# Delta-rule recurrence: the first leaf computed from the contact banks in four pieces, the last decayed W written in place, and P of the even leaves scaled on GpSimd with its products ahead of Q's

## The chip, the cores and the metric

The kernel runs on one core of a Trainium2 chip. The metric is device time in microseconds (us) of one execution, the median of several runs. Engines are named as in the profile: PE is TensorE's matmul, PEld its weight load, DVE is VectorE, ACT is ScalarE, POOL is GpSimd, SPq is the DMA queue of SyncE.

## The reference, cut to what matters

A transformer block on one sequence of 2048 tokens of width 256: layer norm, attention, a residual sum, layer norm, a mixture of experts, a residual sum. The change lies in the attention's recurrence alone (the change also touches how the first stage counts its weight buffers). There are 16 heads; each keeps a 128 by 128 state S that is decayed, corrected and read once a token:

```python
q = silu(dwconv_causal(x @ Wq, ...)); k = ...; v = ...      # (T, 16, 128) each
a = sigmoid(x @ Wa + ba)                                     # (T, 16, 128)
beta = sigmoid(x @ Wb + bb)                                  # (T, 16)
def step(S, t):
    y = einsum('bhvk,bhk->bhv', S, k_t * SCALE)
    err = y - v_t
    S = a_t[..., None] * S - (b_t[..., None] * err)[..., None] * k_t[:, :, None, :]
    o = einsum('bhvk,bhk->bhv', S, q_t)
    return (S, o)
```

## The kernel before, in words

Three stages follow one another. Stage A projects the tokens and convolves them (to about 636 us of the trace), stage B is the recurrence (`recurrence`, 636 to 2758 us), stage C is the feed-forward part. Everything is float32.

**Chunks and leaves.** Stage B walks through 32 chunks (`g`) of 64 tokens for all 16 heads at once, each chunk in 16 leaves (`j`) of 4 tokens. Each engine has its own program, in a fixed order written out by hand; the engines meet through counting semaphores (`wait(engine, count, chunk, k)`), and an engine that waits holds back all that stands behind it in its program. [...]

**Start of a chunk.** PE multiplies the state by the keys and queries of the whole chunk ("contact", 32 matmul records into four PSUM banks, four heads each). `contact_copy` on ACT copies each bank to SBUF, to `P` (the part that belongs to the keys) and `Qs[g % 2]` (the part of the queries). When all four copies are done (`cont`), DVE starts the first leaf.

**A leaf on DVE** (`chunk` in the vector block, L1137 to L1147). A product in place in the leaf's coefficients `NC` (L1137: `left` is the first leaf's P or, from the second leaf on, the sums in the PSUM tile `psM`), a reduction into the solved rows `W` (L1140), and a product with the decays of the leaf (L1147) into `WR` (even leaves), `WT` (odd leaves) or `WC`, which shares its memory with `WE` (the larger merges).

**Behind it.** PE transposes the decayed rows into `psT` (L1723), ACT copies them to `WL`, and PE forms in `psM` what the next tokens need: `WL` times masked products of the keys (`OWN` for an even leaf, `BD` for an odd one, which merges 2, 4 or 8 leaves) plus P and Q of the next tokens, brought in by a product with the identity (L1735, L1739). For an even leaf P and Q are handled together: `pair(g)` is a view of both, DVE scales both by the leaf's decay in one instruction (`scale_leaf`, L1100, 128x128), and two matmuls of 128 columns (two records each, since they are float32) fill `psM` (L1733 and L1735; for the first leaf L1739 and L1741). The next leaf's L1137 waits for both. ACT then copies the rest of P (`rest_copy`, count `prc`) or the leaf's Q (`leaf_q_copy`) out of `psM`.

**DVE's other work in a leaf**, in the order of its program: `add_merged` (L1114), `scale_leaf` (L1100), `scale_leaf_w` (L1105), and then masks, row products and `leaf_solution` of the half chunk to come (L1023), spread over the leaves by hand.

**POOL's program** (`chunk` order in the gpsimd block): `scale_right` (L879 for P and Q of a merge of two leaves, L887 for the larger ones, one instruction for P and one for Q), `scale_left` (L899), `decayed_q` (L850), `gate` (L860), `row_decays` (L830), `block_decays` (L816) and `decayed_w` (L838 to L843). `past(g, j)` is a wait: for an even leaf until DVE has done `scale_leaf_w` (L1105), for an odd one until L1147. In leaf 6 the program reads: `decayed_q`, `gate`, `scale_right(g, 7, (0,))`, `scale_left(g, 5)`, `scale_left(g, 7)`.

**End of a chunk.** After the last leaf ACT copies the last four decayed leaves into `WE`, PE transposes `WE` (L1767), ACT copies that to `WTOK`, PE forms the update of the state (L1665), DVE adds it (L1087), and the next contact begins (L1558). Odd chunks also carry the output projection `wo` of two chunks on PE (L1628, L1688), partly ahead of the merge products of leaf 14.

Every engine's copies on ACT share the line L1244. The kernel text:

Of the kernel before, what the change touches and what calls it, by code (L numbers as in the profile page):

```python
# [10 lines left out]
H, D = 16, 128  # L11
# [57 lines left out]
def project_inputs(nc, ident, x_d, wb_d, bb_d, wpack_d, scr, nbeta_d):  # L69
# [3 lines left out]
    with ctx:  # L73
# [48 lines left out]
        def _(sp):  # L122
# [18 lines left out]
            def heads(t, last):  # L141
                for s in range(2):
# [58 lines left out]
        def _(dve):  # L201
# [45 lines left out]
            c_used[0].start(dve)  # L247
            c_used[1].start(dve)
            with dve.Fori(0, TURNS) as t:
                for s in range(2):  # L250
# [18 lines left out]
                    dve.sem_inc(c_used[s].sem, 1)  # L269

        @block.scalar
        def _(act):
# [43 lines left out]
            for c in (*ag_free, *ca_used):  # L316
                c.start(act)

            with act.Fori(0, TURNS) as t:
                for s in range(2):  # L320
# [35 lines left out]
                    act.sem_inc(ca_used[s].sem, 1)  # L356

        @block.tensor
        def _(pe):
# [31 lines left out]
            w_used[0].start(pe)  # L391
            w_used[1].start(pe)
# [112 lines left out]
def recurrence(nc, ident, scr, nbeta_d, wo_d, lng_d, lnb_d, att_d):  # L505
# [9 lines left out]
    with ctx:  # L515
# [85 lines left out]
        ap = Count(sem("leaf_terms"), J)  # L601
        ws = Count(sem("w_solved"), J, 1, 1)
        wt = Count(sem("w_decayed"), J)
        psc, psc0 = Count(sem("pq_scaled"), JM - 1), Count(sem("leaf_pq_scaled"), JM // 2 + 1)
# [29 lines left out]
        def taken(g, kind, *rest):  # L634
# [13 lines left out]
            return {"contact": (cont, g, n + 1), "ktok": (ktok, g, n + 1), "decay": (stg, g, n + 1),  # L648
# [113 lines left out]
        def _(pool):  # L762
# [125 lines left out]

            def scale_left(g, j):
# [80 lines left out]
        def _(dve):  # L970
# [144 lines left out]

            def chunk(g):
                here, nxt = 2 * g + 1, 2 * g + 2
                more = g + 1 < NCH
                for j in range(J):
# [6 lines left out]
                    if j == 0:  # L1126
                        wait(dve, cont, g, 4)

                        wait(dve, awm, g - 1, 3)
                        wait(dve, wxc, g - 1, 1)  # L1130
                        left = P[:, :, 0:R]
                    else:
                        wait(dve, mps, g, 2 * j - 1)
                        n = merge_of(j - 1)[1]
                        at = H * R * at_p(g) if j % 2 else 0
                        left = psM[:, at:at + H * n].rearrange("p (h t) -> p h t", h=H)[:, :, 0:R]
                    tt(eq[:, :, :, 1:5], eq[:, :, :, 1:5], left.unsqueeze(2).to_broadcast([128, H, R, R]), ALU.mult)\  # L1137
                        .then_inc(ap.sem, 1)
                    wait(dve, ap, g, j + 1)
                    nc.vector.tensor_reduce(W[:, :, lf], eq, AXIS.X, ALU.add).then_inc(ws.sem, 1)  # L1140
                    wait(dve, ws, g, j + 1)
# [1051 lines left out]
```

## Time and profile before

| | |
|---|---|
| median of three runs | 3103.65 us (3093.4 to 3106.2) |
| the profiled execution, span from first to last instruction | 3102.6 us |
| its own time beside the span | the times given are 3106.2, 3103.65 and 3093.4 us; the span lies among them, 1.05 us under the median |
| busy in that span | PE 88%, PEld 60%, DVE 72%, ACT 52%, POOL 44% |
| stage B | 2122 us of the span |

Busy shares are those of the whole span; an engine counts as busy while an instruction of it runs, waiting for an operand port included. A row of the timeline has the start in us, the time it takes in us, the engine, the line of the kernel and the instruction, merged with its like (xN); in brackets is the idle time of the engine before it and who ended it.

### The profile page before, as it was taken

Reading aid. Unit: us, or ns where it says so; the run is one execution under the profiler, and the core shown is the slowest. Engines: PE = TensorE matmul, PEld = TensorE weight load, DVE = VectorE, ACT = ScalarE, POOL = GpSimd, SP = SyncE. Lnnn points to the kernel's source line nnn. Section 1 sums busy time; section 2 is a strip of 40 time slices with the busy share of each in tenths; the row PEclk is TensorE's granted clock in tenths of the full one; section 3 lists DMA queues with packets and bytes.
Section 4 is the critical chain, followed back from the end, with each engine's and each line's share of the span. In section 5 each row is a group of like instructions: output and inputs, shape, how many; then the busy total and the mean of one; then the engine's idle time right before and its main releaser. Section 6 shows DMA issues by size and latency. Waiting matters only on the chain. (4 is left out here: it accounts for less than half of the span.)

```text
span 3102.6 us, 48417 instructions
## 1 busy us (share of the span) xinstructions
PE 2732.2 (88%) x14144; PEld 1863.5 (60%) x14144; DVE 2239.8 (72%) x4680; ACT 1610.3 (52%) x3516; POOL 1377.8 (44%) x1760
## 2 busy tenths in 40 slices
PE   7999999768898888988889888898888888859999
PEld 3555555446666666666666666666666666635555
DVE  6777777677888878888788887888887888623332
ACT  6666666545555555555555555555555555412111
POOL 3666676734544445444454444544445444310000
PEclk9999999989999999999999999999999999979999
DMA  3655556533232232322323223232223222034120
GB/s 124 241 225 206 233 230 239 196 82 67 43 57 42 44 65 47 57 42 43 64 49 57 42 44 59 53 57 42 44 51 61 46 53 43 9 107 109 45 38 14
DMA packets 449883, 261.22 MB, mean 84 GB/s; under 512 B 402672, under 2 KB 414672, under 8 KB 447472
## 3 DMA queue, kind: packets, MB, share of 16 engines
q1 hardware_dynamic: 449664, 258.51, 31.5%
q8 instruction: 112, 1.84, 0.3%
q14 instruction: 107, 0.88, 0.1%
HBM read 153.42 MB, written 105.05 MB: 83 GB/s over the span
## 5 line engine op out<-in xcount | busy, mean ns | idle before, releaser
L265 DVE SCALAR_TENSOR_TENSOR A_acc<-A_psY,A_w,A_acc 128x410 f32<-128x410 f32 (+1 forms) x720 | 419.2, 637 | 151.6 <-ACT A_acc L334 151.6
L405 PE MATMUL A_psY<-A_xT,A_w 128*128 128x413 f32 (+1 forms) x960 | 347.2, 510 | 9.1 <-PE A_psAG L411 7.7
L1244 ACT ACTIVATE B_PQ<-B_psM 128x64 f32<-128x64 f32 (+2 forms) x480 | 125.2, 261 | 441.2 <-DVE B_NC L1137 440.9
L1137 DVE TENSOR_TENSOR B_NC<-B_NC,B_psM 128x256 f32<-128x256 f32 x480 | 200.8, 418 | 182.5 <-PE B_psM L1756 92.8
L192 POOL TENSOR_TENSOR A_outs<-A_outs,A_acc 128x410 f32<-128x410 f32 (+1 forms) x240 | 229.7, 987 | 216.1 <-ACT A_outs L342 216.1
L899 POOL TENSOR_TENSOR B_WT<-B_WT,B_G 128x128 f32<-128x128 f32 (+2 forms) x224 | 143.4, 640 | 371.2 <-ACT B_WT L1244 184.3
L1244 ACT ACTIVATE B_WL<-B_psT 64x128 f32<-64x128 f32 (+3 forms) x480 | 148.5, 309 | 265.6 <-PE B_psT L1723 265.4
L405 PEld LDWEIGHTS A_psY<-A_xT,A_w 128*128 128x128 f32 x960 | 180.2, 189 | 165.5 <-issue 164.2
L1140 DVE TENSOR_REDUCE B_W<-B_NC 128x64 f32<-128x320 f32 x512 | 248.7, 486 | 17.6
L334 ACT ACTIVATE A_acc<-A_psY,A_w 128x410 f32<-128x410 f32 (+1 forms) x240 | 166.1, 692 | 162.9 <-PE A_psY L405 161.2
L879 POOL TENSOR_TENSOR B_PQ<-B_PQ,B_G 128x256 f32<-128x256 f32 x128 | 89.4, 699 | 345.5 <-DVE B_WT L1105 345.5
L1756 PE MATMUL B_psM<-B_BD,B_WL 128*128 128x128 f32 x1536 | 228.2, 288 | 12.4 <-ACT B_WL L1244 4.6
L1756 PEld LDWEIGHTS B_psM<-B_BD,B_WL 128*128 128x128 f32 x1536 | 192.5, 192 | 71.9 <-ACT B_WL L1244 69.5
L411 PE MATMUL A_psAG<-A_xT,A_w 128*128 128x410 f32 (+1 forms) x640 | 233.1, 506 | 0.0
L887 POOL TENSOR_TENSOR B_PQ<-B_PQ,B_G 128x256 f32<-128x256 f32 (+1 forms) x192 | 159.6, 845 | 128.3 <-DVE B_WE L1147 127.6
L1023 DVE TENSOR_TENSOR B_NC<-B_NC,B_TMP 128x384 f32<-128x384 f32 (+1 forms) x192 | 184.7, 962 | 3.3
L411 PEld LDWEIGHTS A_psAG<-A_xT,A_w 128*128 128x128 f32 x640 | 120.9, 189 | 99.6 <-issue 99.6
L1568 PE MATMUL B_ring<-B_KQ,B_KL 128*128 128x256 f32 x512 | 139.5, 396 | 25.4 <-DMA B_KQ<-scr 25.3
L1733 PE MATMUL B_psM<-B_OWN,B_WL 64*128 64x128 f32 x448 | 106.7, 319 | 51.7 <-ACT B_WL L1244 51.7
L2048 ACT ACTIVATE C_act_g<-C_psG 128x512 f32<-128x512 f32 (+1 forms) x56 | 33.4, 597 | 228.3 <-PE C_psU L2103 228.3
L1723 PE MATMUL B_psT<-ident,B_WR 128*64 128x128 f32 x256 | 75.7, 296 | 86.3 <-DVE B_WR L1147 85.1
L850 POOL TENSOR_TENSOR B_SQ<-B_PQ,B_E 128x256 f32<-128x256 f32 x128 | 129.4, 1012 | 47.0 <-DVE B_WT L1147 45.6
(207 smaller groups left out, 6588.4 us busy)
## 6 DMA issues: line engine op xcount, KB each, us to landing
B_KQ<-scr SPq DMA_DIRECT2D x96, 512.0 KB, 6.6
scr<-A_outs SPq DMA_DIRECT2D x48, 615.0 KB, 3.5
scr<-A_outag SPq DMA_DIRECT2D x32, 615.0 KB, 5.2
scr<-A_outs SPq DMA_DIRECT2D x48, 409.0 KB, 2.5
A_xc<-nbeta SPq DMA_DIRECT2D x16, 1024.0 KB, 5.9
B_A<-scr SPq DMA_DIRECT2D x32, 512.0 KB, 4.6
B_C<-scr SPq DMA_DIRECT2D x32, 512.0 KB, 6.3
B_G<-scr SPq DMA_DIRECT2D x32, 512.0 KB, 4.6
```

The lines of the kernel that those rows point to most:

```text
L192: nc.gpsimd.tensor_tensor(o, o, acc[:, p, n % 2, 0:t1 - t0], ALU.mult).then_inc(silu[p].sem, 1)
L265: nc.vector.scalar_tensor_tensor(a, y, w[:, s, col:col + 1], a, ALU.mult, ALU.add)\
L334: nc.scalar.activation(acc[:, p, n % 2, 0:t1 - t0], psY[p][:, y0:y0 + t1 - t0], ACT.Identity, scale=w[:, s, col + HALO:col + HALO + 1], bi ...
L405: last = nc.tensor.matmul(psY[p][:, y0:y0 + HALO + t1 - t0], wp[:, p, kt, :], xT[:, kt, t0:t1 + HALO], start=kt == 0, stop=kt == KT - 1)
L411: last = nc.tensor.matmul(psAG[p][:, 0:t1 - t0], wp[:, A_ + p, kt, :], xT[:, kt, HALO + t0:HALO + t1], start=kt == 0, stop=kt == KT - 1)
L887: tt(x, x, gl.to_broadcast([128, H, n]), ALU.mult).then_inc(psc.sem, 1)
L899: tt(dst, dst, gr, ALU.mult).then_inc(wsc.sem, 1)
L1023: tt(out, in0, in1, op).then_inc(ncs.sem, 1)
L1137: tt(eq[:, :, :, 1:5], eq[:, :, :, 1:5], left.unsqueeze(2).to_broadcast([128, H, R, R]), ALU.mult)\
L1140: nc.vector.tensor_reduce(W[:, :, lf], eq, AXIS.X, ALU.add).then_inc(ws.sem, 1)
L1244: copy = lambda out, in_: nc.scalar.activation(out, in_, ACT.Copy)
L1756: last = mm(psM[:, 512 * q + rs * i:512 * q + rs * (i + 1)], WL[0:rs, 128 * i:128 * (i + 1)], BD[0:rs, bank, col + rs * part:col + rs * (p ...
```

## The change

In stage B:

- **First leaf in pieces.** `first_leaf` on DVE reads each contact bank straight from PSUM (four products of four heads) and reduces after the second and the fourth. ACT's copy of a bank now waits for DVE's product from that bank (`ap`), and a bank is free when both have read it.
- **Last decayed W in place.** L1147 of leaf 15 writes its place in `WE`; ACT's last copy takes three leaves instead of four and no longer waits for leaf 15; PE waits for L1147 instead.
- **Even leaves.** `scale_leaf` on DVE now scales Q alone (128x64). P is scaled on POOL by the new `scale_leaf_p`, placed at eight places of POOL's program (leaves 0, 2, ... 14); for j over 0 it waits for `rest_copy` of leaf j - 1. On PE two products of 128 columns become four of 64: identity times P and `WL` times `OWN` for P, then a semaphore that releases the next leaf, then the same for Q into the other PSUM bank.
- Counts of `ap` and `ws` shift by 3 and 1, with the waits on them.

In stage A the three semaphores on which the weight reload waits (`w_used`, `c_used`, `ca_used`) become one that counts to three.

The diff, cut to its core:

```diff
@@ stage A
-        w_used = [Count(sem(f"A_w_used{s}"), 1, 1, 1) for s in range(2)]
-        c_used = [Count(sem(f"A_c_used{s}"), 1, 1, 1) for s in range(2)]
-        ca_used = [Count(sem(f"A_ca_used{s}"), 1, 1, 1) for s in range(2)]
+        w_used = [Count(sem(f"A_w_used{s}"), 3) for s in range(2)]
...
@@ gpsimd
+            def scale_leaf_p(g, j):
+
+                wait(pool, dec, g, DEC)
+                wait(pool, prc, g, j // 2) if j else wait(pool, cont, g, 4)
+                x = P[:, :, R * (j + 1):R * (j + 2)]
+                tt(x, x, leaf_decay(g)[:, :, j:j + 1].to_broadcast([128, H, R]), ALU.mult).then_inc(psp.sem, 1)
...
                 more = g + 1 < NCH
+                scale_leaf_p(g, 0)
                 past(g, 0)
...
                     decayed_q(g - 1, 1)
+                scale_leaf_p(g, 2)
                 past(g, 2)
...
                     gate(g - 2, 2)
+                scale_leaf_p(g, 4)
                 past(g, 4)
...
                     gate(g - 2, 3)
+                scale_leaf_p(g, 6)
                 scale_right(g, 7, (0,))
                 scale_left(g, 5)
                 scale_left(g, 7)
...
                     row_decays(g + 1, 3)
+                scale_leaf_p(g, 8)
                 past(g, 8)
...
                     row_decays(g + 1, 5)
+                scale_leaf_p(g, 10)
                 past(g, 11)
                 scale_right(g, 11)
+                scale_leaf_p(g, 12)
                 past(g, 12)
                 scale_right(g, 13)
                 scale_left(g, 11)
+                scale_leaf_p(g, 14)
                 past(g, 14)
@@ vector
             def scale_leaf(g, j):
 
-                gl = leaf_decay(g)[:, :, j:j + 1].unsqueeze(1).to_broadcast([128, 2, H, R])
+                gl = leaf_decay(g)[:, :, j:j + 1].to_broadcast([128, H, R])
...
-                    wait(dve, prc, g, j // 2)
                     wait(dve, mq, g, j // 2)
-                x = pair(g)[:, :, :, r0:r0 + R]
+                x = Qs[g % 2][:, :, r0:r0 + R]
...
+            def first_leaf(g, eq):
+
+                for n in range(4):
+                    h = slice(4 * n, 4 * n + 4)
+                    left = take_bank(dve, g, "contact", n)[:].rearrange("p (h q t) -> p h q t", h=4, q=2)[:, :, at_p(g), 0:R]
+                    tt(eq[:, h, :, 1:5], eq[:, h, :, 1:5], left.unsqueeze(2).to_broadcast([128, 4, R, R]), ALU.mult)\
+                        .then_inc(ap.sem, 1)
+                    if n == 1:
+                        wait(dve, awm, g - 1, 3)
+                        wait(dve, wxc, g - 1, 1)
+                    if n % 2:
+                        half = slice(8 * (n // 2), 8 * (n // 2) + 8)
+                        wait(dve, ap, g, n + 1)
+                        nc.vector.tensor_reduce(W[:, half, 0:R], eq[:, half], AXIS.X, ALU.add).then_inc(ws.sem, 1)
...
-                    else:
-                        to = WT[:, j] if j % 2 else WR[:]
+                    elif j < JM:
+                        to = WT[:, j] if j % 2 else WR[:]
+                    else:
+                        wait(dve, tps, g, 12)
+                        to = WE[:, :, R * j:R * (j + 1)]
@@ scalar
                     ps = take_bank(act, g, "contact", i)
+                    wait(act, ap, g, i + 1)
...
-                wait(act, wt, g, J)
+                wait(act, wt, g, JM)
...
-                copy(w_end(12, J), w_leaves(12, J)).then_inc(wec.sem, 1)
+                copy(w_end(12, JM), w_leaves(12, JM)).then_inc(wec.sem, 1)
@@ tensor
                         if p == 0:
+                            wait(pe, psp, g, pair_number(j) + 1)
+                            mm(psM[:, 0:H * n], ident[:], P[:, :, r0:r0 + n], start=True, stop=False)
                             wait(pe, ow, g, 2 if j < 8 else 4)
-                            ...
+                            wait(pe, wl, g, j + 1)
+                            mm(psM[:, 0:H * n], WL[0:rs, 0:128], OWN[0:rs, j // 2, at_p(g), :, R:2 * R],
+                               start=False, stop=True).then_inc(mps.sem, 1)
+                            wait(pe, psc0, g, pair_number(j) + 1)
+                            mm(psM[:, 512:512 + H * n], ident[:], Qs[g % 2][:, :, r0:r0 + n], start=True, stop=False)
+                            mm(psM[:, 512:512 + H * n], WL[0:rs, 0:128], OWN[0:rs, j // 2, at_q(g), :, R:2 * R],
+                               start=False, stop=True).then_inc(mps.sem, 1)
...
                 wait(pe, wec, g, 2)
+                wait(pe, wt, g, J)
```

## Rows read from the trace of the kernel before

**Rows 1.** The page: the span and its instructions

```profile
span 3102.6 us, 48417 instructions
```

**Rows 2.** Stage B: length, busy PE, PEld, DVE, ACT, POOL, granted clock, DMA

```profile
636.00:2758.00 2122.00, 1842.62 (x11466) 1365.79 (x11464) 1671.93 (x3693) 1161.50 (x2724) 970.31 (x1311) 0.98 0.25 48
```

**Rows 3.** DVE's waits, 640 to 2700 us: total us, times, longest

```profile
DVE B_NC L1137 <- ACT B_PQ L1244: 60.8, 24, 2.9
DVE B_NC L1137 <- PE B_psM L1735: 40.3, 51, 1.2
DVE B_NC L1137 <- PE B_psM L1741: 33.0, 32, 3.2
```

**Rows 4.** Timeline: contact, leaf 0 and leaf 1 of a chunk

```profile
1613.62 0.60 ACT L1244 ACTIVATE B_PQ<-B_ring 128x512 f32<-128x512 f32 x1 [0.30 <-PE B_ring L1558]
...
1614.31 0.42 DVE L1137 TENSOR_TENSOR B_NC<-B_NC,B_PQ 128x256 f32<-128x256 f32 x1 [2.65 <-ACT B_PQ L1244]
1614.49 1.14 ACT L1355 ACTIVATE B_BD<-B_ring,B_E 128x128 f32<-128x128 f32 x4 [0.27 <-PE B_ring L1590]
...
1615.29 0.27 DVE L1147 TENSOR_TENSOR B_WR<-B_W,B_E 128x64 f32<-128x64 f32 x1
...
1615.94 0.27 ACT L1244 ACTIVATE B_WL<-B_psT 64x128 f32<-64x128 f32 x1 [0.31 <-PE B_psT L1723]
1616.02 0.67 POOL L879 TENSOR_TENSOR B_PQ<-B_PQ,B_G 128x256 f32<-128x256 f32 x1 [2.09 <-DVE B_WT L1105]
...
1616.36 0.34 PE L1741 MATMUL B_psM<-B_OWN,B_WL 64*128 64x128 f32 x1
...
1616.85 0.42 DVE L1137 TENSOR_TENSOR B_NC<-B_NC,B_psM 128x256 f32<-128x256 f32 x1 [0.96 <-PE B_psM L1741]
...
1617.83 0.27 DVE L1147 TENSOR_TENSOR B_WT<-B_W,B_E 128x64 f32<-128x64 f32 x1
1617.85 1.10 POOL L850 TENSOR_TENSOR B_SQ<-B_PQ,B_E 128x256 f32<-128x256 f32 x1
```

**Rows 5.** Timeline: leaf 6 of that chunk, to the start of leaf 7

```profile
1633.08 1.06 POOL L887 TENSOR_TENSOR B_PQ<-B_PQ,B_G 128x512 f32<-128x512 f32 x1
...
1633.25 0.40 DVE L1137 TENSOR_TENSOR B_NC<-B_NC,B_psM 128x256 f32<-128x256 f32 x1
...
1633.74 0.22 ACT L1244 ACTIVATE B_PQ<-B_psM 128x64 f32<-128x64 f32 x1 [1.49 <-DVE B_NC L1137]
...
1634.09 0.46 POOL L899 TENSOR_TENSOR B_WT<-B_WT,B_G 128x128 f32<-128x128 f32 x1
...
1634.20 0.47 DVE L1147 TENSOR_TENSOR B_WR<-B_W,B_E 128x64 f32<-128x64 f32 x1
...
1634.97 0.29 DVE L1100 TENSOR_TENSOR B_PQ<-B_PQ,B_E 128x128 f32<-128x128 f32 x1
...
1637.28 0.42 DVE L1137 TENSOR_TENSOR B_NC<-B_NC,B_psM 128x256 f32<-128x256 f32 x1
```

**Rows 6.** Timeline: L1147 of leaf 1 in another chunk, beside POOL

```profile
2138.01 1.10 DVE L1147 TENSOR_TENSOR B_WT<-B_W,B_E 128x64 f32<-128x64 f32 x1
2138.02 0.97 POOL L850 TENSOR_TENSOR B_SQ<-B_PQ,B_E 128x256 f32<-128x256 f32 x1
```

**Rows 7.** Groups by form, 640 to 2700 us: count, busy us, mean ns, idle

```profile
L1105 DVE TENSOR_TENSOR B_WT<-B_WR,B_E 128x64 f32<-128x64 f32 x254 | 55.3, 218 | 0.2
...
L816 POOL TENSOR_TENSOR B_G<-B_G 128x64 f32<-128x64 f32 x31 | 9.2, 298 | 2.4
```

**Rows 8.** Timeline: merge products of leaf 12 and start of leaf 13, odd chunk

```profile
1659.79 0.46 PE L1733 MATMUL B_psM<-B_OWN,B_WL 64*128 64x128 f32 x2 [0.45 <-ACT B_WL L1244]
...
1660.70 0.42 DVE L1137 TENSOR_TENSOR B_NC<-B_NC,B_psM 128x256 f32<-128x256 f32 x1 [0.99 <-PE B_psM L1735]
```

**Rows 9.** Timeline: ACT's last WE copy, even chunk; PE's transposes, odd chunk

```profile
1605.15 0.42 ACT L1244 ACTIVATE B_WE<-B_WT 128x256 f32<-128x256 f32 x1
...
1671.84 1.04 PE L1767 MATMUL B_psM<-ident,B_WE 128*128 128x128 f32 x8
```

More of the change, by code:

```diff
@@ L246, in _ @@
                 tap[p].start(dve)
-            c_used[0].start(dve)
-            c_used[1].start(dve)
             with dve.Fori(0, TURNS) as t:
@@ L268, in _ @@
                     dve.wait_ge(tap[2].sem, tap[2].at(t, 3 * (s + 1) * NTA))
[L269 removed]
+                    dve.sem_inc(w_used[s].sem, 1)
         @block.scalar
@@ L315, in _ @@
             nc.scalar.activation(nbeta[:], beta[:], ACT.Copy, scale=-SCALE * SCALE).then_inc(nbeta_sb, 1)
-            for c in (*ag_free, *ca_used):
+            for c in ag_free:
                 c.start(act)
@@ L390, in _ @@
             pe.wait_ge(beta_sb, T // 512)
-            w_used[0].start(pe)
-            w_used[1].start(pe)
             with pe.Fori(0, TURNS) as t:
@@ L600, in recurrence @@
         cont = Count(sem("contact_copied"), 4)
-        ap = Count(sem("leaf_terms"), J)
-        ws = Count(sem("w_solved"), J, 1, 1)
+        ap = Count(sem("leaf_terms"), J + 3)
+        ws = Count(sem("w_solved"), J + 1, 1, 1)
         wt = Count(sem("w_decayed"), J)
+        psp = Count(sem("leaf_p_scaled"), JM // 2 + 1)
         psc, psc0 = Count(sem("pq_scaled"), JM - 1), Count(sem("leaf_pq_scaled"), JM // 2 + 1)
@@ L647, in taken @@
                 return (am if n else atc, (g - 3) // 2, 1),
-            return {"contact": (cont, g, n + 1), "ktok": (ktok, g, n + 1), "decay": (stg, g, n + 1),
+            if kind == "contact":
+                return (cont, g, n + 1), (ap, g, n + 1)
+            return {"ktok": (ktok, g, n + 1), "decay": (stg, g, n + 1),
                     "update": (stu, g, n + 1), "oc": (oc, g - 1, n + 1),
@@ L1126, in chunk @@
                     if j == 0:
[L1127 to L1131, printed above, removed]
+                        first_leaf(g, eq)
                     else:
@@ L1134, in chunk @@
                         n = merge_of(j - 1)[1]
[L1135 to L1141, printed above, removed]
+                        left = psM[:, 0:H * n].rearrange("p (h t) -> p h t", h=H)[:, :, 0:R]
+                        tt(eq[:, :, :, 1:5], eq[:, :, :, 1:5], left.unsqueeze(2).to_broadcast([128, H, R, R]), ALU.mult)\
+                            .then_inc(ap.sem, 1)
+                        wait(dve, ap, g, j + 4)
+                        nc.vector.tensor_reduce(W[:, :, lf], eq, AXIS.X, ALU.add).then_inc(ws.sem, 1)
+                    wait(dve, ws, g, j + 2)
                     p, n, _ = merge_of(j)
@@ L1297, in leaf_diagonals @@
                         wait(act, zeros, 0, NZERO + 1)
-                    wait(act, ws, g - 1, 8 * h + 8)
+                    wait(act, ws, g - 1, 8 * h + 9)
                     copy(flat[:, :, 1], ones[:].to_broadcast([128, HJ2])).then_inc(nc0.sem, 1)
@@ L1363, in rest_copy @@
                 wait(act, mps, g, 2 * j + 1)
-                wait(act, ap, g, j + 2)
+                wait(act, ap, g, j + 5)
                 copy(P[:, :, r0 + R:r0 + n], m[:, :, R:n]).then_inc(prc.sem, 1)
             def leaf_q_copy(g, j):
-                m = psM[:, H * R * at_q(g):H * R * (at_q(g) + 1)].rearrange("p (h t) -> p h t", h=H)
+                m = psM[:, 512:512 + H * R].rearrange("p (h t) -> p h t", h=H)
                 wait(act, mps, g, 2 * j + 2)
-                wait(act, ap, g, j + 2)
+                wait(act, ap, g, j + 5)
                 copy(Qs[g % 2][:, :, R * (j + 1):R * (j + 2)], m).then_inc(mq0.sem, 1)
@@ L1716, in chunk @@
                         wait(pe, wl, g, j)
-                        wait(pe, ap, g, j + 1 if j else 0)
+                        wait(pe, ap, g, j + 4 if j else 0)
                         for i in range(tiles):
@@ L1761, in chunk @@
                         run_job(g, job)
-                wait(pe, ap, g, J)
+                wait(pe, ap, g, J + 3)
                 wait(pe, mq, g, JM // 2)
```

17 lines of the change are left out of this document (2 added, 15 removed).

## The prediction, made before the changed kernel ran

> **What bounds the kernel now.** I read the page first: the profiled execution spans 3102.6 us [rows 1], 1.05 us under the median of 3103.65 us, so I sum against 3102.6 and carry the sum to 3103.65 unchanged. The view by stretch puts 2122 us into stage B [rows 2]. The edit of stage A's semaphores leaves the same three conditions in front of the same load, so I cost it at 0, and all that follows is stage B: 32 chunks, 66.3 us each if the stretch is divided evenly. A gain of 1 us in a chunk is 32 us, 1%.
>
> Busy shares don't say what bounds the chunk: DVE is busy for 1671.93 of 2122 us, PE for more, and both have idle time [rows 2]. The view of waits shows where DVE idles ahead of L1137, the head of each leaf. Three rows bear on this change. It waits for the copies of the contact banks, in total 60.8 us; for the first leaf's pair of products (L1741) in 32 chunks of 32, 33.0 us; and for the later even leaves' pair (L1735) 51 times, 40.3 us [rows 3]. There are 7 such leaves in each of 32 chunks, 224 in all. So in 173 of them DVE is not waiting for these products: it still works on masks or leaf solutions. That is the first thing to see: the reordered products can help in 83 places at most.
>
> The second is a coupling of DVE and POOL. In leaf 6 POOL's L899 runs from 1634.09 to 1634.55, and DVE's L1147 takes 0.47 us and ends at 1634.67, 0.12 us after it [rows 5]. The same form takes 0.27 us in leaves 0 and 1 [rows 4]. In another chunk L1147 takes 1.10 us and ends at 2139.11, where POOL's L850 ended at 2138.99: again 0.12 us later [rows 6]. But L1137, which reads PSUM, takes 0.40 us under POOL's L887, no longer than its 0.42 elsewhere [rows 4, 5]. So a DVE product of two SBUF tiles waits until the POOL instruction is through, a product from PSUM doesn't. L1147, L1100, L1105 and L1023 are of the first kind, and L1147 is the head of the chain to PE's transposes.
>
> The Trainium skill (SBUF — State Buffer, section "Who interferes with whom") has this rule: a DVE instruction with two SBUF inputs and a GpSimd instruction that reads SBUF exclude each other for a whole instruction. The rows agree that one waits for the other. By the rule alone a blocked instruction would also take its whole time after the other's end, an estimated 0.1 us more than the 0.12 us of the rows; with four blockings in each of 32 chunks that would be some 13 us more in the sum below. I use the rows.
>
> **First leaf in pieces.** The last copy starts at 1613.62 after 0.30 us of idleness on PE, so the last bank is full at about 1613.5; L1137 starts at 1614.31 [rows 4]. A piece of 128x64 costs about 0.22 us (L1105, the same size, 218 ns [rows 7]). Product and reduction take 1615.29 - 1614.31 = 0.98 us up to L1147, 0.42 of it the product [rows 4]; for half a reduction I take 0.32 of the other 0.56, with a fixed part that doesn't halve. New L1147: it starts at 1613.6 + 0.22 + 0.32, with two short waits at about 1614.25, and is ready at 1614.5, where it was ready at 1615.56: 1.06 us earlier on DVE.
>
> That isn't what leaf 1 gains. ACT must first copy the last bank, now behind DVE's piece: 1613.9 to 1614.5. Then stand its four masked copies (1.14 us, L1355), until about 1615.7, and only then the copy to WL, which starts at 1615.94 now [rows 4]. 0.24 us is left. The product that the next leaf waits for has 64 columns instead of 128: from L1741's start to L1137 is 0.49 us [rows 4], I take 0.42. Together leaf 1 starts 0.31 us earlier, at 1616.54.
>
> What is late next is POOL. Its chain L879, L887 twice, L850 starts when L1105 of leaf 0 has ended, and L850 starts 1.83 us after L879 (1616.02, 1617.85). In the same chunk DVE's L1147 starts at 1617.83, 0.02 us ahead, and it is POOL that waits: L850 takes 1.10 instead of the 0.97 of rows 6 [rows 4, 6]. With the change L1105 ends at about 1615.2 (last copy 1614.5, then Q's 0.22, P on POOL 0.30 between, W's 0.22), 0.7 us earlier, while leaf 1 gains only 0.31. L850 then starts at about 1617.15, ahead of L1147, which is ready at 1616.54 + 0.98 = 1617.52. L850 ends at 1618.13, L1147 at 1618.25, and it ends at 1618.10 now. I enter a loss of 0.10 us a chunk. Bounds: a gain of 0.31 (no blocking), a loss of 0.52 (the 0.83 that rows 6 shows for a full blocking, less 0.31).
>
> **P on POOL.** One instruction of 128x64 costs POOL 298 ns [rows 7] and takes from DVE 0.29 - 0.22 = 0.07 us (L1100 against L1105) [rows 5, 7]. POOL has idle time in stage B, 2122 - 970 us [rows 2], so the 8 x 0.3 = 2.4 us a chunk fit; their place is what counts. `scale_leaf_p` waits for ACT's copy of P, which in leaf 6 starts at +0.49 us after L1137 and takes 0.22 [rows 5]. So it begins at about +0.9 us, just where L1147 stands (+0.95). In leaves 2, 4, 8 and 12 the copy is later or longer, L1147 is first, and P fits in behind it: no loss, and 0.07 us gained where DVE sets the time (I count leaves 2 and 4: 0.14 a chunk). In leaves 10 and 14 L1147 may end 0.1 us later, against the same 0.07: a loss of 0.03 together.
>
> **Leaf 6 is the place that decides.** Now `scale_right(g, 7, (0,))` runs from 1633.08 to 1634.14 and `scale_left(g, 5)` to 1634.55: under L1137 and the reduction, which don't mind, and only 0.20 us of it blocks L1147 [rows 5]. With the change both stand behind `scale_leaf_p(g, 6)`, which waits until about 1634.15. In terms of L1137's start: P +0.92 to +1.22, L1147 ends at +1.34 (it ends at +1.42 now), L887 +1.3 to +2.35. L1114 reads PSUM and passes; L1100 has to wait until +2.35 and ends at +2.47; then L899 until +2.9 and L1105 until +3.02. Now L1100 starts at +1.72, and with 0.22 for each of the two that follow L1105 is done at about +2.16. That is 0.86 us later for the leaf solutions behind it. Leaf 7's L1137 follows DVE's own work with no idle time (no bracket at 1637.28 [rows 5]), so nothing hides it. I enter a loss of 0.85. Bounds: 0 (POOL gets through earlier), and 1.3, the sum of 1.06 and 0.46 less the 0.2 that blocks already [rows 5].
>
> **Products of P first.** In leaf 12 of an odd chunk L1733 starts at 1659.79 and L1137 at 1660.70: 0.91 us behind the copy to WL [rows 8]. With identity times P already in the bank, one product of 64 columns is left, 0.42 to 0.49 (from L1741 [rows 4]): 0.45 us earlier. DVE idles 0.99 us there [rows 8]. In odd chunks, however, PE's own queue sets the end: `wo` and its rest lie in leaves 11 to 14, and the transposes of WE follow with no idle time on PE [rows 9]. The merge issues 8 records instead of 4, so PE's queue isn't shorter, and I take 0 for the odd chunks. In even chunks I take 0.30 for leaf 12, which averages to 0.15. In all, the 51 waits of 0.79 us [rows 3] with at most 0.45 each bound this gain at 23 us, 0.72 a chunk.
>
> **Last W in place.** ACT's copy starts at 1605.15 with no idle time ahead of it [rows 9], so ACT sets it, not L1147. It shrinks from four leaves to three, by a tenth of 0.42 us or so; in odd chunks PE is late anyway [rows 9]. 0.02 on average; at most 0.42.
>
> **Sum.** -0.10 + 0.14 - 0.03 - 0.85 + 0.15 + 0.02 = -0.67 us a chunk, a loss; times 32 it is 21 us. In the first chunk there is less work beside the leaves, and I round to 20: 3103.65 + 20 = 3124 us, 0.65% slower.
>
> **The rivals.**
>
> *POOL's queue doesn't collide (faster).* It takes only leaf 6: if P's turn comes in the gaps and L887 with L899 is through before L1100, the loss of 0.85 is gone, and leaf 1 keeps its 0.31. Then 0.31 + 0.14 + 0.15 + 0.02, and 0.15 more where leaf 14 gains in even chunks: 0.77 a chunk, 25 us, 3079 us. For it: the 93.8 us of waits for contact and first pair are there [rows 3], and the chain is long. Against it: the blocking shows to 0.01 us in two places. It decides from where leaf 6 loses less than 0.3 us. Chance 0.22.
>
> *Gains and losses cancel (same).* Leaf 6 loses about half of what I enter (0.4), or leaf 1 wins its 0.31 while leaf 6 loses 0.85: -0.2 a chunk, 3110 us; or the work of leaves 6 and 7 is partly caught up where DVE waits for PE in leaf 8. Here the change does little, as 173 of 224 even leaves don't wait for the products. Chance 0.30.
>
> *More collisions (much slower).* POOL is shifted against DVE in every leaf, and L1147 of leaf 1 pays the full 0.52 and leaf 6 1.3: -1.7 a chunk, 54 us, 3158 us. For it: rows 6 shows 0.83 us lost by a single crossing. Against it: POOL idles much of each chunk [rows 2]. Chance 0.12.
>
> My forecast has 0.36. Its own range is 3110 to 3138. A difference of 0.5% (16 us) is about what can be told from no change here. The cases give faster 0.22, same 0.30 and slower 0.48. The range that leaves out no more than 2 in 10 runs from 3080 to 3148 us.
>
> **What would show it.** In the changed profile L1137's idle time before leaf 1 falls, and L1147 of leaf 1 takes more than 0.27 us in most chunks. In leaf 6 L887 starts after `scale_leaf_p`, at about +1.3 us instead of -0.17, L1100 or L1105 takes over 0.5 us, and leaf 6 lasts about 4.9 us instead of 4.03. The waits on ACT's contact copies (60.8 us) are replaced by waits on PE's contact products. The waits for L1735 don't vanish by more than 23 us. I am wrong if leaf 6 keeps its 4.03 us, or if PE's queue in the odd chunks gets shorter.

## The result, and the profile after

The changed kernel took 3150.72 us (median of 4 runs, 3147.51 to 3153.97), the kernel before beside it 3099.97 us: a ratio of 1.0164, 95% interval 1.0149 to 1.0179. It is slower by 51 us. I had forecast 3124 us and a range up to 3148; the direction was right, the size 2.5 times too small, and the time lies outside the range.

The page of the changed kernel, its span and busy times:

```profile
span 3145.8 us, 51018 instructions
...
PE 2853.9 (91%) x15168; PEld 2028.0 (64%) x15168; DVE 2290.5 (73%) x4808; ACT 1599.2 (51%) x3516; POOL 1467.3 (47%) x2016
```

PE has 1024 records more than before and 122 us more busy time (2732.2 before), DVE 51 us more, POOL 90 us more for its 256 new products. The spans of the two profiled executions, 3102.6 and 3145.8 us, are 43 us apart and not 51, at a granted clock of 0.976 and 0.975. The changed kernel's other three runs had a lower clock (0.970 to 0.974). At 0.975 it took 3147.51 us, and the kernel before, in runs beside the experiments, 3100.29 and 3103.64 us, so at the same clock 44 to 47 us remain of the 51. Whether the lower clock comes from the change is not shown.

DVE's waits in stage B, from 640 to 2700 us (total us, times, longest), where [rows 3] had 60.8 us for the contact copies and 73.3 us for the first pair and the pairs behind it:

```profile
DVE B_NC L1156 <- PE B_psM L1757: 63.3, 60, 1.6
DVE B_NC L1016 <- ACT B_X L1266: 32.9, 62, 1.1
DVE B_rdev L1075 <- PE B_ring L1639: 25.5, 30, 2.2
DVE B_NC L1130 <- PE B_ring L1581: 24.2, 47, 0.7
```

The wait ahead of the first leaf fell from 77.6 to 24.2 us: beside the 60.8 us of [rows 3], which are 24 of the chunks, the view of before has seven more waits of 2.4 us on average at the same place (16.8 us, put down to "issue"). The waits for the products of the even leaves fell by 10 us. Three waits grew that I had not looked for. The one for L1062, DVE's mask of the own products, which waits for PE, was 17.7 us in the kernel before and is 39.7 now (`DVE B_OWN L1062 <- PE B_ring L1591`). The other two are shown above: L1016 is DVE's row product, which waits for ACT's copy of what PE formed, and L1075 is the reciprocal in leaf 13, which waits for PE. In the kernel before they were 16.5 us and 3.2 us. DVE's wait for `wo` at L1085, in leaf 15 of the odd chunks, grew from 10.6 to 22.9 us.

From DVE's records the length of each leaf can be worked out: the distance between the starts of successive reductions of DVE (L1140 before; for a first leaf in pieces, its second reduction), as a mean over chunks 4 to 29. "Start" is leaf 15 of a chunk, its end and leaves 0 and 1 of the next.

```
us a chunk   before after  leaf6 leaf1 P_DVE pairs Qearly Q+6  Q+6+1 first+last  +leaf1  pairs+6+1
start        16.21  16.91  16.89 16.79 16.92 16.13 16.43 16.38 16.03 15.99       15.70   15.72
leaves 2-5   13.87  13.74  13.73 13.84 13.78 13.63 13.62 13.63 13.63 13.86       13.87   13.63
leaf 6        4.02   4.63   3.78  4.63  4.04  4.63  4.63  3.78  3.78  4.03        4.04    3.78
leaves 7-9   12.03  11.95  12.01 11.95 12.09 12.03 11.95 11.96 11.96 12.03       12.04   12.03
leaves 10-14 18.81  19.28  19.42 19.34 19.68 18.97 18.77 18.96 18.77 18.92       18.85   18.87
chunk        64.93  66.50  65.82 66.56 66.50 65.40 65.41 64.71 64.17 64.84       64.50   64.04
```

After against before: start +0.70, leaves 2 to 5 -0.13, leaf 6 +0.61, leaves 7 to 9 -0.08, leaves 10 to 14 +0.47. That is 1.57 us a chunk in these 26 chunks. Over all chunks, from leaf 1 of the first to leaf 15 of the last, the two traces differ by 43 us, as much as the spans. The columns behind the second are experiments below, in this order: the swap in leaf 6; the decayed Q product ahead of leaf 0; P on DVE; pairs on PE; Q early; Q early with the swap; and with both moves; the first leaf in pieces and the last W alone; the same with the move ahead of leaf 0; pairs with both moves. Differences in time between runs are differences of medians; the kernel before, timed beside each group of runs, had medians from 3097.86 to 3100.97 us. The ratios are formed from runs side by side and differ from the quotients of the medians by up to 0.0008.

**Leaf 6** looks as forecast. The timeline of the changed kernel, which answers to [rows 5] (start, us, engine):

```profile
1654.61 0.41 DVE L1156 TENSOR_TENSOR B_NC<-B_NC,B_psM 128x256 f32<-128x256 f32 x1
...
1655.48 0.33 POOL L889 TENSOR_TENSOR B_PQ<-B_PQ,B_E 128x64 f32<-128x64 f32 x1 [1.05 <-ACT B_PQ L1266]
1655.57 0.36 DVE L1169 TENSOR_TENSOR B_WR<-B_W,B_E 128x64 f32<-128x64 f32 x1
1655.76 1.09 POOL L882 TENSOR_TENSOR B_PQ<-B_PQ,B_G 128x512 f32<-128x512 f32 x1
1655.85 0.28 DVE L1123 TENSOR_TENSOR B_PQ<-B_PQ,B_psM 128x128 f32<-128x128 f32 x1
1656.16 0.77 DVE L1109 TENSOR_TENSOR B_PQ<-B_PQ,B_E 128x64 f32<-128x64 f32 x1
1656.82 0.45 POOL L901 TENSOR_TENSOR B_WT<-B_WT,B_G 128x128 f32<-128x128 f32 x1
1656.86 0.49 DVE L1114 TENSOR_TENSOR B_WT<-B_WR,B_E 128x64 f32<-128x64 f32 x1
...
1659.23 0.40 DVE L1156 TENSOR_TENSOR B_NC<-B_NC,B_psM 128x256 f32<-128x256 f32 x1
```

Each product of two SBUF tiles ends 0.08 to 0.12 us behind POOL's: L1169 at 1655.93 (POOL 1655.81), L1109 at 1656.93 (1656.85), L1114 at 1657.35 (1657.27). L1123, with an input from PSUM, takes its usual 0.28 us under POOL. The two scalings, 0.22 us each when free, take 0.77 and 0.49.

**Leaf 12** shows what I had not priced. PE's products behind the copy to WL in an odd chunk, kernel before (its weight loads, since they show when the next work could be issued):

```profile
1659.75 0.29 PEld L1733 LDWEIGHTS B_psM<-B_OWN,B_WL 64*128 64x128 f32 x2 [0.80 <-issue]
1660.17 0.30 PEld L1735 LDWEIGHTS B_psM<-B_PQ,ident 128*128 128x128 f32 x2
1660.39 0.73 PEld L1590 LDWEIGHTS B_ring<-B_KQ,B_KL 128*128 128x128 f32 x4
```

and in the changed kernel, with what hangs on it in leaf 13:

```profile
1681.91 0.29 PEld L1757 LDWEIGHTS B_psM<-B_OWN,B_WL 64*128 64x128 f32 x2 [0.39 <-issue]
...
1682.27 0.30 PEld L1760 LDWEIGHTS B_psM<-B_PQ,ident 128*128 128x128 f32 x2
...
1682.38 0.42 DVE L1156 TENSOR_TENSOR B_NC<-B_NC,B_psM 128x256 f32<-128x256 f32 x1 [0.65 <-PE B_psM L1757]
...
1682.63 0.29 PEld L1761 LDWEIGHTS B_psM<-B_OWN,B_WL 64*128 64x128 f32 x2
...
1682.99 0.73 PEld L1613 LDWEIGHTS B_ring<-B_KQ,B_KL 128*128 128x128 f32 x4
...
1684.06 0.23 PE L1639 MATMUL B_ring<-ident,B_E 8*128 8x8 f32 x1
...
1684.32 0.21 DVE L1075 RECIPROCAL B_rdev<-B_ring 128x8 f32<-128x8 f32 x1 [0.70 <-PE B_ring L1639]
```

From the first product with WL to the next work on PE it was 1660.39 - 1659.75 = 0.64 us; now it is 1682.99 - 1681.91 = 1.08 us, 0.36 for each of three products. The same distance is 0.63 and 1.09 us as a median over chunks 4 to 29 in each of leaves 2, 6, 8, 12 and 14. In leaf 0, where one product stood behind WL before and three do now, it is 0.16 and 0.85 us. In leaves 4 and 10 it hardly grows (0.83 and 0.85). In leaf 10 PE isn't idle ahead of the product with WL, so P's identity product delays this one, and the distance leaves that out. DVE starts leaf 13 earlier behind the copy to WL (0.47 us behind L1757's load, where it was 0.95), but the work behind the merge is 0.44 us later on PE, and DVE then waits 0.70 us for it at L1075. The reordering moves the wait and adds to it.

### The profile page after: what moved, and what is told of

Its sections match the earlier page's. It is cut to its first block and busy times, and to the rows that moved or that the text cites. A ratio compares the mean times of both kernels' runs of the same rounds, so it can differ in the third digit from the quotient of the medians.

```text
span 3145.8 us, 51018 instructions
## 1 busy us (share of the span) xinstructions
PE 2853.9 (91%) x15168; PEld 2028.0 (64%) x15168; DVE 2290.5 (73%) x4808; ACT 1599.2 (51%) x3516; POOL 1467.3 (47%) x2016
## 5 line engine op out<-in xcount | busy, mean ns | idle before, releaser
L1156 DVE TENSOR_TENSOR B_NC<-B_NC,B_psM 128x256 f32<-128x256 f32 x480 | 199.4, 415 | 149.4 <-PE B_psM L1776 79.6
L889 POOL TENSOR_TENSOR B_PQ<-B_PQ,B_E 128x64 f32<-128x64 f32 x256 | 91.4, 357 | 434.0 <-ACT B_PQ L1266 429.6
L1159 DVE TENSOR_REDUCE B_W<-B_NC 128x64 f32<-128x320 f32 x480 | 233.2, 486 | 16.5
L1591 PE MATMUL B_ring<-B_KQ,B_KL 128*128 128x256 f32 x512 | 141.1, 399 | 25.7 <-DMA B_KQ<-scr 25.7
L1757 PE MATMUL B_psM<-B_OWN,B_WL 64*128 64x64 f32 x512 | 107.4, 290 | 37.5 <-ACT B_WL L1266 36.3
```

## The experiments

**The order on GpSimd in leaf 6.** A swap of two lines in the changed kernel:

```diff
-                scale_leaf_p(g, 6)
                 scale_right(g, 7, (0,))
+                scale_leaf_p(g, 6)
```

> The changed kernel with one swap in GpSimd's program: in leaf 6 the scaling of P for the merge of leaf 7 (128x512) goes ahead of the scaling of leaf P, as it stood before. Theory (GpSimd in DVE's way): leaf 6 falls from 4.63 us to about 4.0, 0.6 us a chunk, 19 us in all: 3131 us, 1.010 of the kernel before. Rival (the time of leaf 6 is PE's or DVE's own, the order on GpSimd doesn't matter): leaf 6 stays at 4.6 us and the time at 3145 to 3155.

Measured: 3130.79 us, 1.0095 (1.0072 to 1.0117), 20 us less than the changed kernel. Leaf 6, timeline:

```profile
1647.23 1.05 POOL L882 TENSOR_TENSOR B_PQ<-B_PQ,B_G 128x512 f32<-128x512 f32 x1
...
1647.46 0.41 DVE L1156 TENSOR_TENSOR B_NC<-B_NC,B_psM 128x256 f32<-128x256 f32 x1
...
1648.33 0.33 POOL L889 TENSOR_TENSOR B_PQ<-B_PQ,B_E 128x64 f32<-128x64 f32 x1
1648.42 0.35 DVE L1169 TENSOR_TENSOR B_WR<-B_W,B_E 128x64 f32<-128x64 f32 x1
...
1649.00 0.23 DVE L1109 TENSOR_TENSOR B_PQ<-B_PQ,B_E 128x64 f32<-128x64 f32 x1
```

The long product runs under L1156 and the reduction again, which don't mind it, and L1109 is back at 0.23 us. Leaf 6 falls by 0.85 us to 3.78 (under the 4.02 of before, since DVE scales Q alone). Leaf 7 falls by 0.69 as well, but leaf 8 grows by 0.74. Of this, 0.39 us a chunk are DVE's waits for PE (its mask of the own products, L1062, from 39.7 to 52.3 us in all), and 0.31 are a new crossing: with leaf 8 reached earlier, its decay product L1169 meets `row_decays` on POOL and takes 0.58 us instead of 0.27. So POOL's order is one cause, and behind leaf 6 both PE and POOL take back what leaf 7 gains.

**GpSimd's first decayed Q product ahead of leaf 0**, to take it out of the way of leaf 1's decay product:

```diff
+                if g:
+                    decayed_q(g - 1, 0)
                 scale_leaf_p(g, 0)
                 past(g, 0)
...
-                if g:
-                    decayed_q(g - 1, 0)
                 scale_left(g, 1)
```

> The changed kernel with GpSimd's first decayed Q product of a chunk (128x256, about 0.98 us) moved from leaf 1 into the idle time ahead of leaf 0, before the scaling of the first leaf's P. Theory (crossing in leaf 1): the decay product of leaf 1 takes 0.27 us again instead of 0.81, leaf 1 falls by 0.5 us, 17 us in all: 3134 us, 1.011. Rival (the crossing only moves): the decay product of leaf 0 is blocked instead, by up to 0.9 us, and since PE and ACT are later than DVE there only part of it shows: 3140 to 3150 us.

Measured: 3154.77 us, 1.0175 (1.0152 to 1.0197): no gain. The rows of leaf 1 say why:

```profile
1638.68 1.08 PE L1672 MATMUL B_ring<-B_QS,B_source 64*128 64x256 f32 x7
...
1639.13 0.27 DVE L1169 TENSOR_TENSOR B_WT<-B_W,B_E 128x64 f32<-128x64 f32 x1
1639.69 0.14 PEld L1746 LDWEIGHTS B_psT<-ident,B_WT 128*128 128x128 f32 x1 [0.33 <-DVE B_WT L1169]
...
1639.97 1.23 DVE L1071 TENSOR_TENSOR B_WX<-B_ring,B_WX 128x1024 f32<-128x1024 f32 x1 [0.57 <-PE B_ring L1672]
```

The crossing in leaf 1 is gone, L1169 takes 0.27 us and is done at 1639.40. But PE is busy with L1672 to 1639.76, behind the four products of leaf 0, and transposes at 1639.69; L1071 waits 0.57 us for it. Neither expectation named this: PE was as late as the crossing. The rival was right in its first half: L1169 of leaf 0 now takes 0.73 us on average (chunks 4 to 29) where it took 0.27. It costs little there, since leaf 0 grows from 2.93 to 2.98 us only. Both are taken up again below.

**P on DVE, PE's new order kept.** `scale_leaf` as before, no `scale_leaf_p`, and PE waits for the one scaling in place of the two:

```diff
-                            wait(pe, psp, g, pair_number(j) + 1)
+                            wait(pe, psc0, g, pair_number(j) + 1)
                             mm(psM[:, 0:H * n], ident[:], P[:, :, r0:r0 + n], start=True, stop=False)
...
-                            wait(pe, psc0, g, pair_number(j) + 1)
```

> The changed kernel with P and Q of the even leaves scaled together on DVE as before, nothing of it on GpSimd; PE still forms P's products first, as four products of 64 columns. Theory (two causes, GpSimd's crossings and PE's longer queue): leaf 6 is back at 4.0 us (19 us), leaves 10 to 13 keep their loss of 0.6 us against the kernel before, leaf 1 keeps its crossing: 3130 us, 1.010. Rival (GpSimd alone is the cause): only leaf 1's 0.5 us is left, which the gains in leaves 2, 8, 10 and 12 outweigh: 3095 us or less. Rival (PE alone): about 3150 us.

Measured: 3156.89 us, 1.0185 (1.0160 to 1.0210). My expectation of 3130 fell. Leaf 6 is back at 4.04 us, but leaves 10 to 14 grow from 19.28 to 19.68. Leaf 12 of an even chunk:

```profile
1618.28 0.41 PE L1747 MATMUL B_psM<-B_PQ,ident 128*128 128x64 f32 x2 [0.52 <-DVE B_PQ L1102]
...
1618.61 0.43 PE L1750 MATMUL B_psM<-B_OWN,B_WL 64*128 64x64 f32 x2
1618.97 0.43 PE L1752 MATMUL B_psM<-B_PQ,ident 128*128 128x64 f32 x2
...
1619.34 0.43 PE L1753 MATMUL B_psM<-B_OWN,B_WL 64*128 64x64 f32 x2
...
1619.70 1.37 PE L1606 MATMUL B_ring<-B_KQ,B_KL 128*128 128x256 f32 x4
```

Now even P's product with the identity waits for DVE (0.52 us), and all four products stand behind the copy to WL: 1619.70 - 1618.28 = 1.42 us. With P's scaling off GpSimd the kernel is as slow, which "GpSimd alone" can't explain. It points to PE's queue, and suggests what P on GpSimd is good for: it brings P early enough for PE's idle time.

**The first leaf in pieces and the last W in place alone**, all even leaves as before:

> The kernel before with the first leaf in pieces and the last decayed W in place alone; all even leaves as before, with two products of 128 columns and both parts scaled on DVE. Theory (the first leaf's gain is lost to the crossing in leaf 1): leaf 1 takes 0.5 us more, the start of the chunk 0.2 to 0.3 less, the rest is unchanged: 3108 us, 1.002 to 1.004. Rival (these two parts are the gain of the change, the even leaves its loss): 0.3 us a chunk faster, 3090 us.

Measured: 3099.76 us, 1.0001 (0.9990 to 1.0012), somewhat below the expected 1.002 to 1.004. The start of the chunk is 15.99 us instead of 16.21, with leaf 1 at 2.92 instead of 2.55: its decay product takes 0.66 us on average where it took 0.30, and 0.81 in the changed kernel. The rival of 3090 us falls. Against this run the change of the even leaves alone adds 0.92 us to the start: 0.82 in leaf 15 (10.09 to 10.91), 0.15 in leaf 1 and -0.05 in leaf 0.

**PE's pairs as before, P still on GpSimd.** The four products become two of 128 columns again, with P and Q side by side in one bank (the readers' columns as before):

```diff
-    mm(psM[:, 0:H * n], ident[:], P[...]) ... four products of 64 columns
+    mm(psM[:, 0:2 * rs], WL[0:rs, 0:128], OWN[0:rs, j // 2, :, :, R:2 * R], start=True, stop=False)
+    wait(pe, psp, g, pair_number(j) + 1)
+    wait(pe, psc0, g, pair_number(j) + 1)
+    mm(psM[:, 0:2 * rs], ident[:], pair(g)[:, :, :, r0:r0 + n], start=False, stop=True).then_inc(mps.sem, 2)
```

> The changed kernel with PE's products of the even leaves as before (two of 128 columns, P and Q together, one release), while P is still scaled on GpSimd and Q on DVE. Theory (PE's queue: the four products of 64 columns hold PE 0.45 us longer behind each copy to WL, and this shows in leaves 1, 11 and 13): leaf 11 is back at 4.3 us, leaf 13 at 4.0, leaf 6 keeps its 4.6: 3118 us, 1.006. Rival (GpSimd's products and the crossings are the cause, PE only follows): leaves 11 and 13 stay at 4.8 and 5.0 us, 3145 us or more.

Measured: 3115.52 us, 1.0044 (1.0027 to 1.0061), against the expected 3118; 35 us less than the changed kernel, with GpSimd untouched. Leaf 11 is back at 4.31 us (from 4.83) and leaf 13 at 4.05 (from 4.91), leaf 6 keeps its 4.63. The rival falls. But the largest part is where I hadn't expected it: of the 1.10 us a chunk, 0.77 are in leaf 15 (10.14 instead of 10.91), and leaf 1 gains only 0.07. Leaf 15 of an odd chunk in the changed kernel, and then with the pairs:

```profile
1691.84 0.49 DVE L1159 TENSOR_REDUCE B_W<-B_NC 128x64 f32<-128x320 f32 x1
1694.86 0.42 DVE L1085 TENSOR_TENSOR B_att<-B_att,B_ring 128x256 f32<-128x256 f32 x1 [1.63 <-PE B_ring L1711]
1695.10 1.04 PE L1788 MATMUL B_psM<-ident,B_WE 128*128 128x128 f32 x8
```

```profile
1676.61 0.49 DVE L1160 TENSOR_REDUCE B_W<-B_NC 128x64 f32<-128x320 f32 x1
1678.76 0.42 DVE L1085 TENSOR_TENSOR B_att<-B_att,B_ring 128x256 f32<-128x256 f32 x1 [0.76 <-PE B_ring L1712]
1678.99 1.04 PE L1794 MATMUL B_psM<-ident,B_WE 128*128 128x128 f32 x8
```

From the products of leaf 14 to the transposes of `WE` PE has no idle time in either, so its longer queue moves them one for one: they begin 1695.10 - 1691.84 = 3.26 us behind the leaf's reduction, and 2.38 with the pairs. Leaf 15 of the odd chunks is 11.40 and 10.52 us. In the even chunks, where PE has some idle time, it is 10.42 and 9.75.

**The same four products, Q's identity product ahead of the wait for WL.** Nothing is removed, one product and its wait change their place:

```diff
                             mm(psM[:, 0:H * n], ident[:], P[:, :, r0:r0 + n], start=True, stop=False)
+                            wait(pe, psc0, g, pair_number(j) + 1)
+                            mm(psM[:, 512:512 + H * n], ident[:], Qs[g % 2][:, :, r0:r0 + n], start=True, stop=False)
                             wait(pe, ow, g, 2 if j < 8 else 4)
                             wait(pe, wl, g, j + 1)
```

> The changed kernel with one product moved on PE: identity times Q goes ahead of the wait for WL, directly behind identity times P, so that behind the copy to WL stand only the two products with WL. Same products, same records. Theory (PE's queue): behind WL PE is held some 0.45 us instead of 1.09, leaf 11 falls from 4.83 to 4.3 us and leaf 13 by 0.6 or more, leaf 6 keeps its loss: 3115 us, 1.006. Rival (the count of records, not their place, sets PE's time): no change, 3145 to 3155 us. Rival (Q's scaling on DVE is now in P's way): leaf 8, where DVE scales Q late, grows by 0.2 us.

Measured: 3110.43 us, 1.0033 (1.0022 to 1.0044), expected 3115. Leaf 12 of an odd chunk:

```profile
1666.46 0.33 PE L1754 MATMUL B_psM<-B_PQ,ident 128*128 128x64 f32 x2
...
1666.63 0.39 PE L1756 MATMUL B_psM<-B_PQ,ident 128*128 128x64 f32 x2
...
1667.08 0.40 PE L1759 MATMUL B_psM<-B_OWN,B_WL 64*128 64x64 f32 x2
1667.32 0.38 PE L1761 MATMUL B_psM<-B_OWN,B_WL 64*128 64x64 f32 x2
...
1667.63 1.13 PE L1613 MATMUL B_ring<-B_KQ,B_KL 128*128 128x256 f32 x4
...
1668.95 0.21 DVE L1075 RECIPROCAL B_rdev<-B_ring 128x8 f32<-128x8 f32 x1 [0.19 <-PE B_ring L1639]
```

Both identity products run while ACT copies WL. Behind it PE is held 1667.63 - 1667.08 = 0.55 us, and L1075 waits 0.19 us instead of 0.70. The number of products is that of the changed kernel, so it is mainly not their number but their place behind the copy to WL that cost. Over all chunks the wait at L1075 falls from 25.5 to 11.1 us, those at L1016 and L1062 to 17.1 and 25.5. The third expectation, a loss of 0.2 us in leaf 8, shows as 0.06 (3.34 to 3.40), and as 0.16 in leaf 10 (3.25 to 3.41).

**Both cures**, Q early and the swap in leaf 6:

> The kernel of the run above with the swap on GpSimd in leaf 6 as well (128x512 for the merge of leaf 7 ahead of the scaling of leaf P). With PE's queue out of the way the whole 1.5 us that the swap gained in leaves 6 and 7 should stay, where 0.7 of it was given back in leaf 8. Theory: 3075 to 3090 us, 0.994. Rival (the two gains don't add up, leaf 8 waits for PE as before): 3100 to 3110 us.

Measured: 3089.07 us, 0.9954 (0.9940 to 0.9968): 62 us less than the changed kernel, where the single cures gave 20 and 40. They add up, and the time is at the upper end of what was expected, but not as I had it: leaf 7 is back at 6.02 us and leaf 8 at 3.41, so of the 1.5 us that the swap had gained in leaves 6 and 7 only the 0.85 of leaf 6 stays.

**And the decayed Q product ahead of leaf 0** on top:

> The same with GpSimd's first decayed Q product moved ahead of leaf 0 as well, the move that gained nothing while PE was late in leaf 1. Theory (the crossing in leaf 1 shows once PE isn't late): another 0.2 to 0.4 us a chunk, 3070 to 3080 us. Rival (blocked in leaf 0 instead, or PE still late): no gain against the run above.

Measured: 3083.85 us, 0.9952 (0.9935 to 0.9969), 4 us above the expected range. Leaf 1 falls from 3.06 to 2.53 us, so the move that brought nothing with PE late shows in the trace now; leaf 0 takes 0.15 more, as its own decay product is blocked now (0.81 us instead of 0.27). The chunk is 0.54 us shorter in the trace, 0.35 of it in the start; the two intervals of the ratios overlap, so they don't tell this gain apart.

**The same move without the even leaves' change:**

> The kernel before with the first leaf in pieces and the last W in place (as in the run that came out equal to the kernel before), and GpSimd's first decayed Q product moved ahead of leaf 0. Theory (the crossing in leaf 1 eats what the first two parts gain): leaf 1 falls from 2.92 to 2.5 us, 13 us in all: 3087 us, 0.996. Rival (blocked in leaf 0 instead): 3100 us.

Measured: 3087.39 us, 0.9963 (0.9949 to 0.9977), as expected. Leaf 1 is at 2.53 us instead of 2.92, and the start at 15.70 instead of 15.99. Here the crossing in leaf 1 is shown by itself: it had eaten most of what the first leaf in pieces gains. It isn't avoided but moved to leaf 0, whose decay product takes 0.77 us now, and where DVE waits for PE behind it: leaf 0 grows by 0.07 only. The move alone, in the kernel before, was not run; leaf 1 is at 2.55 us there already.

**The last W in place alone:**

> The kernel before with the last decayed W in place alone. Theory (ACT sets the start of its last copy, and PE is late in odd chunks): 0.1 us in the even chunks, 0 in the odd ones, 3098 to 3101 us. Rival (the copy stood in the way in every chunk): 0.4 us a chunk, 3088 us.

Measured: 3102.62 us, 1.0014 (1.0004 to 1.0024): no gain, by the interval slower by 0.04 to 0.24%, and above the expected 3098 to 3101 us; its chunk is 64.99 us against 64.93. The rival of 0.4 us a chunk falls.

**A version that beats both**: pairs as before on PE, P on GpSimd, and both moves on GpSimd:

> The changed kernel with PE's pairs of products as before, and both moves on GpSimd (leaf 6 and ahead of leaf 0). P is scaled on GpSimd. Theory (the places' gains add): 3115 less 0.8 us a chunk for leaf 6 and 0.4 for leaf 1, 3077 us, 0.993; so P ahead of Q is not what brings the gain. Rival (PE's order with Q early is the better one): 3090 us or more, above the 3084 of that order.

Measured: 3073.27 us, 0.9924 (0.9907 to 0.9940), 77 us less than the changed kernel and the fastest of the study. It has the two parts of the change that gain, the first leaf in pieces and P scaled off DVE, and not P's products ahead of Q's. That P on GpSimd gains once POOL's order is right shows against the run with the first leaf in pieces, the last W in place and the move ahead of leaf 0: 3073.27 against 3087.39 us, a chunk of 64.04 against 64.50 us, and the intervals of the two ratios lie apart. Compared with the run of Q early and both moves, the difference of 0.28% is at the edge of what the intervals tell, and that run had a lower granted clock (0.971 against 0.980 when profiled).

## Why the prediction was wrong

**The step that failed** is "Products of P first", where it says: "The merge issues 8 records instead of 4, so PE's queue isn't shorter, and I take 0 for the odd chunks", and enters a gain of 0.15. I priced only when P's part is ready, and treated PE's queue behind it as no matter. Measured, PE is held 1.08 us behind the copy to WL instead of 0.64 in five of the eight even leaves, 0.85 instead of 0.16 in leaf 0, and this reaches DVE where it waits for work of PE that stands behind the merge: L1016 in leaf 11, L1075 in leaf 13, and above all the end of the chunk in leaf 15. The 0 for the odd chunks fails by its own premise: the prediction itself says that PE's queue sets the end there and that the transposes of `WE` follow with no idle time, so a longer queue had to delay them, and it does, by 0.88 us against the run with the pairs. Leaves 10 to 14 lose 0.47 us a chunk where I had forecast a gain of 0.12. That PE's order is the cause is shown from two sides: the pairs take 35 us off, the early Q with all products kept takes 40 off. Part of these is the granted clock, which was lower in the changed kernel's runs (0.970 to 0.975 against 0.975 to 0.980); at 0.975 or 0.976 the pairs took 3117.89 and the early Q 3114.29 and 3118.16 us, 29 to 33 less than the 3147.51 of the changed kernel. By the leaves the pairs are worth 1.10 us a chunk, of the 1.57 that were lost. I had read DVE's waits for the products themselves and counted 173 leaves of 224 without one; what those leaves wait for next, a job of PE behind the merge, I didn't follow.

**Leaf 6** was right in mechanism and place, and mis-sized upward: a loss of 0.85, measured 0.61 a chunk (L1109 blocked to +2.32 and L1114 to +2.74 us, where I had +2.47 and +3.02). The swap gave 20 us.

**Leaf 1 and the first leaf**: I entered a net loss of 0.10 with bounds of +0.31 and -0.52. The whole start of the chunk lost 0.70, beyond the bound, because two things coincide: the crossing with L850 that I described (L1169 of leaf 1 takes 0.81 us on average over chunks 4 to 29, 0.30 before), and PE's queue, which I didn't. With the pairs the start is 16.13 us, with the pairs and no crossing in leaf 1 15.72: 0.78 for PE's order, nearly all of it in leaf 15, and 0.41 for the crossing. In leaf 1 the two hide one another: removing the crossing alone brings 0.11 us (2.96 from 3.07) and the pairs alone 0.07, both together 0.54. So the first leaf in pieces, with the last W in place, gains 0.5 us a chunk once both are out of its way (15.70 against 16.21), where I had 0.31 at best.

**P on POOL.** Leaves 2 to 5 gained 0.13 us with 0.14 forecast, but that is luck. Leaf 2 gained 0.14 and leaf 4 0.12 where I had 0.07 each, leaves 3 and 5 gave 0.06 and 0.07 back, and leaf 2's part is the work of PE's order: it is there with P on DVE as well (3.34 us) and gone with the pairs (3.48). With PE's pairs P on POOL takes 0.23 us off these leaves (13.63 against 13.86). In leaf 10 too it is the faster P product, not POOL, that counts: 3.25 us instead of 3.48, and 3.26 with P on DVE, given back in leaf 11. One product costs POOL 0.33 us alone and 357 ns on average, where I had taken 298 from another product.

**The last W in place** was right: nothing (0.02 forecast). **The rival** of work being caught up in leaf 8 was seen once, in the swap run, in the other direction: a gain in leaves 6 and 7 was given back there. The rival "more collisions" had the nearest number, -1.7 us a chunk and 3158 us, and this too is luck: its price is 1.3 us in leaf 6, which lost 0.61, and it has nothing of PE's queue. Its terms with the rest of the sum as it stands give -1.54 us and 3153; the 0.15 of P's products was left out without a word.

What stays open: leaf 0 in the start of the chunk was not divided further into ACT's part and PE's. Leaf 3 has a crossing of the same kind in the kernel before already (its decay product takes 0.67 us on average); what it costs is not known, since in the run with P on DVE the product takes 0.28 us and the leaf is no shorter than in the changed kernel (3.57 us). And why a product of 64 columns holds PE for 0.36 us in one order and 0.24 in another was not tried by itself.

## What to carry to other kernels

If a wait for a result is shortened by splitting the work, look at what stands behind the split work on the same engine, and who waits for that: here the early release started leaf 13 0.48 us sooner behind the copy to WL, and the queue behind it, 0.44 us later, took more. Fill the engine's idle time ahead of the last input with all that doesn't need it, rather than only with the part that is urgent. When two engines exclude each other, as DVE's products of two SBUF tiles and POOL's do here, place the long one under work that doesn't mind (reductions, inputs from PSUM), and don't let a new short instruction with a late wait stand ahead of it.

## What the runs showed of the hardware

- A float32 product of 64 columns held PE for 0.36 us (L1757 to L1760 to L1761 to the next work), where the two products of 128 columns in the kernel before held it for 0.42 and 0.22 us, by the starts of the weight loads: here half the columns didn't take half the time. The weight loads, two records of 0.18 to 0.19 us for each product, are the same for either width.
- Two products with the same weights into two PSUM banks stood 0.24 us apart (L1759, L1761), while identity product and WL product into the same columns stood 0.36 us apart (L1760, L1761), with no wait for another engine between them in either case. This was seen beside other changes and not isolated.
- In leaf 6 DVE and POOL take turns: at the end of each of POOL's three instructions one of DVE's ends, 0.08 to 0.12 us after it, so a long product of POOL holds back one instruction of DVE and not all. It goes the other way too: POOL's product of P takes 0.33 us alone and 0.45 beside L1169 of leaf 12 (L889 at 1680.23, L1169 at 1680.21). The Trainium skill (SBUF — State Buffer, section "Who interferes with whom") calls the pair of ports that the two share an exclusive lock, under which the other one fully blocks. The trace agrees that the blocked one doesn't end first, but its free time of 0.22 us isn't paid in full behind the other's end.
- The order in which PE's records start isn't always that of the program: in the kernel before a record of L1649 starts at 1616.49, between the two of L1741 (1616.36 and 1616.54), and in the changed kernel one of L1672 at 1638.12, between the two of L1761 (1638.11 and 1638.27).
